# Mean squares and inverse roots of blocks 2 to 7: from TensorE to GpSimd and VectorE

## The chip, the cores and the metric

One core of a Trainium2 chip runs the whole program as one launch. The metric is the device time of that launch in microseconds; the median of three runs is compared. The engines have a queue each and run side by side: TensorE (PE in the profile; its weight loads are PEld), VectorE (DVE), ScalarE (ACT), GpSimd (POOL). SyncE (SP) issues nearly all the transfers. They meet at semaphores only.

## The reference, cut to what matters

`x` has 2 batches of 2048 tokens and 512 features. Two layers follow each other:

```python
# layer 0
scale = cond @ norm_w.T + 1.0
ms = jnp.mean(x * x, axis=-1, keepdims=True)
h = x * (scale[:, None, :] * jax.lax.rsqrt(ms + EPS))
u = h @ up_w.T                      # 512 -> 4096
val, gate = jnp.split(u, 2, axis=-1)
h = val * jax.nn.gelu(gate, approximate=False)
y = act_quant(h) @ weight_quant(down_w).T + x
# layer 1: down = relu(y @ Wd_b.T + bd); out = y + down @ Wu_b.T + bu
```

`Wd_b` and `Wu_b` are weights that are made from the condition by two large products with `cond`. The change concerns the second and third line of layer 0 alone: the mean square of each token, and the inverse root that all 512 features of the token are multiplied by.

## The kernel before, in words

Features lie on the 128 partitions and tokens along the free dimension. The 4096 tokens are 8 blocks of 512 (`TB`); two blocks make a stage `s` (0 to 3). The up projection of a stage is done in 16 steps `j`, 64 in all (`n = 16 s + j`, called quads in the code). A quad is seven products of block matrices (a Winograd-like scheme, `product(n, p)` in the order 1, 5, 3 of the quad before, 6, 4 of the quad before, 2, 7); a product is six 128x128 by 128x512 matmuls in f16, since each operand is split in a high and a low half. Between the quads stand the groups for the layer-1 weights (`adapter_group`, 16 matmuls), the down projection of the stage before (`down`), and small products.

The order of the work on each engine is written out by hand, in one loop over the quads for each engine. What a quad needs from the others:

- `product(n, 5)` waits in stage 0 for `u_low(n, 1)` on VectorE (the low half of part 1 of the weights), and behind every second quad for `exponents` (the scales of the next two quads' weights).
- `product(n, 7)` waits for `seed_c(n)` on VectorE.
- In stage 0 the split weights of quad `j` are made while quad `j - 1` runs: GpSimd makes four sums of weight blocks (`weight_sums(j)`, four additions of 128x256), ScalarE rounds them (`u_high(j, 1)` from the first two sums, `u_high(j, 3)` from the last two), VectorE makes the low halves (`u_low`). From stage 1 on they are loaded from DRAM.
- ScalarE's order in quad `n` of stage 0 is `seed_b(n)`, `keep_p5(n)`, `u_high(n+1, 0)`, `gate2(n-1)`, `u_high(n+1, 1)`, `absolute2(n-1)`, `row_sums(n+3)`, `absolute1(n-1)`, `u_high(n+1, 2)`, `u_high(n+1, 3)`, `gate1(n)`.
- VectorE's order in it ends with `u_low(n+1, 0)`, `multiply2(n-1)`, `seed_c(n)`, `multiply1(n-1)`, `running_max2(n-1)` (which waits for `absolute2`), `running_max1(n-1)` (which waits for `absolute1`), `u_low(n+1, 1)`, `val2(n)`.

The rows of the next stage are prepared in quads 2 to 15 of the stage that runs. For each of its two blocks: ScalarE squares the four groups of features and VectorE adds them up in `res[:, 2, :]` (`add_squares`). Behind quad 6 (first block) and quad 9 (second), `stat` on TensorE sums over the partitions, by four f32 matmuls of the squares with a column of ones, into four columns of `e_ps`, with the tokens now on the partitions; `mean_square` on VectorE reads them at the start of the next quad, and product 5 waits for that. At the end of quad 10, `rsqrt` makes the roots of both blocks, 128 x 4 each. Behind quads 11 and 12, `spread_rs` on TensorE turns them back by four transposes into one 128x512 PSUM bank, in which every partition has the root of every token, and `x_scaled` on VectorE multiplies the block by it at the start of quads 12 and 13.

GpSimd has one queue: `weight_sums` of all 16 steps in `SUM_ORDER`, and then `all_h(s)`, two `partition_all_reduce` over the running maxima, once a stage. Blocks 0 and 1 have a path of their own, which the change leaves alone.

Of the kernel before, what the change touches and what calls it, by code (L numbers as in the profile page):

```python
# [165 lines left out]
STAT = {6: 0, 9: 1}  # L166
ROOTS = 10
SPREAD = {11: 0, 12: 1}
NEXT_X = {2: 0, 5: 1}
MID_AT = {49: 0, 52: 1, 55: 2}  # L170
UP_AT = {n + 1 + k // 2: (i, (k, k + 1)) for n, i in MID_AT.items() for k in (0, 2)}
# [6 lines left out]
def side_work(n):  # L178

    s, j = divmod(n, NP)  # L180
    work = [("dw", g) for g in groups_of_quad(n)]
    if n == 0:
        work.append(("bounds", 0))
    if s + 1 < NSB:
        if j in SPREAD:
            work.append(("rs", 2 * s + 2 + SPREAD[j]))
    if s > 0 and Y_FIRST <= j < Y_FIRST + 4:
        for m in (2 * (j - Y_FIRST), 2 * (j - Y_FIRST) + 1):
            work.append(("y", 2 * (s - 1) + m // KD, m % KD))
    if n in MID_AT:  # L190
        work.append(("mid", MID_AT[n]))
    if n in UP_AT:
        i, ks = UP_AT[n]
        work += [("up", i, k) for k in ks]
    return work
# [20 lines left out]
def build(nc, x, cond, norm_w, up_w, down_w, Wd, bd, Wu, bu, Wdd, bdd, Wdu, bdu, out):  # L216
    aux = aux_plan()
    aux_keys = list(aux)
    with ExitStack() as ctx:
# [46 lines left out]

        d_raw = res[:, 0:2, :].rearrange("p a t -> p (a t)")
        norm_raw = stage[:, 0, :]
        cs_pow = exps[:, 0:B]
        h_half = h_ring[:, :, :].rearrange("p s t -> p (s t)").bitcast(F16).rearrange(  # L270
            "p (s t) -> p s t", s=SLOTS)
# [143 lines left out]
        s_sqp = sem("s_sqp")  # L415
        s_rs = sem("s_rs")
        s_spread = sem("s_spread")
        s_xs = sem("s_xs")
        s_t = [sem(f"s_t_sum{m}") for m in range(7)]
        s_thi = sem("s_thi")  # L420
# [12 lines left out]
        s_wq = sem("s_wq")  # L433
        s_mean = sem("s_mean")
        s_down_total = sem("s_down_total")
        s_stat = sem("s_stat")
        s_stage = sem("s_stage")
        s_l1w = sem("s_l1w")
        s_chain = sem("s_chain")
# [7 lines left out]
        def bank_free(key):  # L447
            kind, i = key[:2]
            at = ADAPTERS.index(i) if kind in ("mid", "up") else 0
            return {  # L450
                "scale": (s_cs, 1),
                "stat": (s_ms, 1),
                "rs": (s_xs, KD * (i + 1)),
                "total": (s_top, 1),
                "bounds": (s_top, bound_count(3)),
                "dw": (s_stage, i + 1),
                "y": (s_x1, KD * i + key[-1] + 1),
                "mid": (s_relu, at + 1),
                "up": (s_out, KD * at + key[-1] + 1),
            }[kind]  # L460
# [246 lines left out]
        @block.gpsimd  # L707
        def _(pool):
            pool.memset(ones[:, :], 1.0).then_inc(s_const, 1)
            pool.memset(ident[:, :], 1.0).then_inc(s_const, 1)  # L710
            pool.wait_ge(s_const, 2)
            pool.affine_select(out=ident[:, :], in_=ident[:, :], compare_op=ALU.is_equal, fill=0.0,
                               base=0, pattern=[[-1, P]], channel_multiplier=1).then_inc(s_const, 1)

            def a_block(j, half, which):
                return u_raw(j)[:, 2 * half:2 * half + 2, P * which:P * which + P]

            def weight_sums(j):

                pool.wait_ge(s_u[j % 4], 16 * (j // 4 + 1))  # L720
                if j == 2:

                    aux_ready(pool, "dw", 2)
                elif j == 4:
                    aux_ready(pool, "dw", 3)
                elif j == 0:

                    pool.wait_ge(s_seed_c, 1)
                elif j >= 3:
                    if j == 6:  # L730
                        pool.wait_ge(s_sums_lo, 2)
                    pool.wait_ge(s_ulo, part_count(j - 2, 3))
                s1, s2, s3, s4 = (s_sum(j, n, n + 1).rearrange("p (k m) -> p k m", k=2)
                                  for n in range(4))
                pool.tensor_tensor(s1, a_block(j, 0, 0), a_block(j, 1, 0), ALU.add)\
                    .then_inc(s_us, 1)
                pool.wait_ge(s_us, sum_count(j, 1))
                pool.tensor_tensor(s2, s1, a_block(j, 0, 1), ALU.subtract).then_inc(s_us, 1)
                pool.tensor_tensor(s3, a_block(j, 0, 1), a_block(j, 0, 0), ALU.subtract)\
                    .then_inc(s_us, 1)  # L740
                pool.wait_ge(s_us, sum_count(j, 2))
                pool.tensor_tensor(s4, a_block(j, 1, 1), s2, ALU.subtract).then_inc(s_us, 1)

            def all_h(s):

                if s:
                    pool.wait_ge(s_x1, 2 * KD * s)
                for t, s_max in ((1, s_max2), (0, s_max1)):
                    pool.wait_ge(s_max, NP * (s + 1))
                    if s == NSB - 1 and t == 0:  # L750

                        pool.wait_ge(s_step, 1)
                    pool.partition_all_reduce(yscale[:, TB * t:TB * t + TB],  # L753
                                              hmax[:, TB * t:TB * t + TB], P, AR.absmax)\
                        .then_inc(s_ma[t], 1)


            pool.wait_ge(s_rs, 2)
            for j in SUM_ORDER:
                weight_sums(j)  # L760
            for n in range(NP, NQ, NP):
                all_h(n // NP - 1)
            all_h(NSB - 1)

        @block.scalar
        def _(act):
# [6 lines left out]
            def square(i, k):  # L773
                act.wait_ge(s_x[i % 2], 16 * (i // 2))
                if k == 0 and i % 2:
                    act.wait_ge(s_stat, i - 2)
                if k > 1:
                    act.wait_ge(s_sqp, (KD - 1) * (i - 2) + k - 1)
                act.activation(res[:, 2 + (k > 0), :], x_sb[:, i % 2, k, :], ACT.Square)\
# [239 lines left out]
        def _(pe):  # L1019
# [16 lines left out]
            def product(n, p):  # L1036
# [14 lines left out]
                elif p == 5:  # L1051
# [3 lines left out]
                        pe.wait_ge(s_top, bound_count(2))  # L1055
                    if n - 1 in BOUND_QUADS:
                        pe.wait_ge(s_top, bound_count(n + 1))
                    if stat_of_quad(n - 1) is not None:
                        pe.wait_ge(s_ms, stat_of_quad(n - 1) + 1)
                    if n - 1 == MEAN_QUAD:  # L1060
                        pe.wait_ge(s_mean, 1)
                    ps = e_ps
# [76 lines left out]
                                   start=True, stop=True)  # L1139
                mm.then_inc(s_aux, 1)  # L1140

            def stat(i):
                ps = e_ps[:, 2:2 + NT] if i else take("stat", 0)
                if i == 0:
                    pe.wait_ge(s_sqr, KD - 1)
                    sq = h_ring[:, 0, 0:TB]
                else:
                    pe.wait_ge(s_sqp, (KD - 1) * (i - 1))
                    sq = res[:, 2, :]
                for t in range(NT):  # L1150
                    mm = pe.matmul(ps[:, t:t + 1], sq[:, P * t:P * t + P], ones[:, 0:1],
                                   start=True, stop=True)
                mm.then_inc(s_stat if i else s_aux, 1)

            def stat1(part):

# [6 lines left out]
                mm.then_inc(s_stat1, 1)  # L1163

            def spread_rs(i):
                ps = spread_first[i] if i < 2 else take("rs", i)
                pe.wait_ge(s_rs, i + 1)
                for t in range(NT):
                    col = NT * (i % 2) + t
                    mm = pe.transpose(ps[:, P * t:P * t + P],  # L1170
                                      rs[:, (i // 2) % 2, col:col + 1].to_broadcast([P, P]),
                                      ident[:, :])
                mm.then_inc(s_spread if i < 2 else s_aux, 1)

            def down(i, k):
                ps = take("y", i, k)
# [68 lines left out]
                               cond_sb[:, 0:B], start=True, stop=True)  # L1245
            mm.then_inc(s_aux, 1)
            pe.wait_ge(s_const, 1)
            stat(0)
            stat1(0)
            first_bounds()  # L1250
            pe.wait_ge(s_const, 3)
# [21 lines left out]
            for n in range(NQ):  # L1273
# [9 lines left out]
                    product(n, 7)  # L1283
                for g in groups_of_quad(n):
                    adapter_group(g)
                if stat_of_quad(n) is not None:
                    pe.wait_ge(s_p5sb, n)
                    stat(stat_of_quad(n))
                if n in BOUND_QUADS:
                    pe.wait_ge(s_p5sb, n)  # L1290
                    bounds(n + 2, n + 3, e_ps).then_inc(s_total, 1)
# [1 line left out]
                    pe.wait_ge(s_p5sb, n)  # L1293
                    down_total()
                for key in side_work(n)[len(groups_of_quad(n)):]:
                    if key[0] == "rs":
                        spread_rs(key[1])
                    elif key[0] == "bounds":
                        bounds(3, 3, take(*key)).then_inc(s_aux, 1)
                    elif key[0] == "y":  # L1300
                        down(key[1], key[2])
# [46 lines left out]
        def _(dve):  # L1348
# [108 lines left out]
            def mean_square(i):  # L1457
# [6 lines left out]
                        total, e_ps[:, 0:2 * NT].rearrange("p (k t) -> p t k", k=2),  # L1464
                        AX_X, ALU.add))
                elif i:
                    dve.wait_ge(s_stat, i - 1)
                    total = e_ps[:, 2:2 + NT]
                else:
                    aux_ready(dve, "stat", 0)  # L1470
                    total = bank("stat", 0)[:, 0:NT]
# [3 lines left out]
            def rsqrt(i, count=1):  # L1475
# [4 lines left out]
                if i == 0:  # L1480
# [19 lines left out]
                dve.scalar_tensor_tensor(out=y, in0=t, scalar=1.5 * 1.5, in1=y,  # L1500
                                         op0=ALU.add, op1=ALU.mult).then_inc(s_rs, count)

            def x_scaled(i, ks=range(KD)):
                if i < 2:
                    dve.wait_ge(s_spread, i + 1)
                    roots = spread_first[i]
                else:
                    aux_ready(dve, "rs", i)
                    roots = bank("rs", i)
                b = i // 4  # L1510
                for k in ks:
                    xk = x_sb[:, i % 2, k, :]
# [251 lines left out]
            for n in range(1, NQ):  # L1764
# [15 lines left out]
                for key in side_work(n - 1):  # L1780
                    if key[0] == "y":
                        residual(key[1], (key[2],))
                    elif key[0] == "rs":
                        x_scaled(key[1])
                    elif key[0] == "up":
                        finish(key[1], key[2])
                if j == 0:
                    t_low(s, T3)
                if s + 1 < NSB:
# [56 lines left out]
                    t_low(s + 1, B21)  # L1846
                if j == ROOTS and s + 1 < NSB:
                    rsqrt(2 * s + 2, 2)
                if n == 12:
                    down_mean()  # L1850
            n = NQ - 1
# [92 lines left out]
```

## Time and profile before

| | us |
|---|---|
| median of three runs | 850.98 (849.87, 850.98, 851.22) |
| span of the profiled execution, first to last instruction | 847.8 |
| TensorE busy | 834.7 |
| VectorE busy | 605.6 |
| ScalarE busy | 388.4 |
| GpSimd busy | 74.3 |

The times of whole runs hold some microseconds more than the span, before the first and after the last instruction; the profile tells nothing of those. Busy times add up each engine's instructions; a busy TensorE is not yet a TensorE at its peak, since matmuls overlap and their ends are modelled. What a matmul costs in the flow is read from the distance of two starts.

### The profile page before, as it was taken

Reading aid. Unit: us, or ns where it says so; the run is one execution under the profiler, and the core shown is the slowest. Engines: PE = TensorE matmul, PEld = TensorE weight load, DVE = VectorE, ACT = ScalarE, POOL = GpSimd, SP = SyncE. Lnnn points to the kernel's source line nnn. Section 1 sums busy time; section 2 is a strip of 40 time slices with the busy share of each in tenths; the row PEclk is TensorE's granted clock in tenths of the full one; section 3 lists DMA queues with packets and bytes.
Section 4 is the critical chain, followed back from the end, with each engine's and each line's share of the span. In section 5 each row is a group of like instructions: output and inputs, shape, how many; then the busy total and the mean of one; then the engine's idle time right before and its main releaser. Section 6 shows DMA issues by size and latency. Waiting matters only on the chain.

```text
span 847.8 us, 11801 instructions
## 1 busy us (share of the span) xinstructions
PE 834.7 (98%) x3982; PEld 366.9 (43%) x3982; DVE 605.6 (71%) x904; ACT 388.4 (46%) x633; POOL 74.3 (9%) x79
## 2 busy tenths in 40 slices
PE   6999999999999999999999999999999999999998
PEld 4334444444444444444444444444444444444443
DVE  5998787989877765658776656668975664445986
ACT  5778887775454532237454542126333332224000
POOL 0363332202000000002000000000200000000100
PEclk9999999999999999999999999999999999999999
DMA  9879988665999843377889754436246444432232
GB/s 342 333 269 339 348 285 300 235 224 209 323 350 373 305 149 117 116 255 274 294 308 335 270 200 134 151 106 211 84 133 217 137 162 141 140 117 77 99 123 76
DMA packets 64426, 183.49 MB, mean 216 GB/s; under 512 B 7024, under 2 KB 8304, under 8 KB 64368
## 3 DMA queue, kind: packets, MB, share of 16 engines
q1 hardware_dynamic: 64080, 182.48, 61.7%
q8 instruction: 33, 0.54, 0.2%
q10 hardware_dynamic: 288, 0.26, 0.1%
q14 instruction: 25, 0.20, 0.1%
HBM read 152.31 MB, written 29.36 MB: 214 GB/s over the span
## 4 chain that ended last, share of the span: by engine, by line
PE 93%; DVE 1%; issue 0%; DVEq 0%
PE aux_ps L1182 10%; PE b_ps L1082 9%; PE b_ps L1086 9%; PE b_ps L1084 9%; PE a_ps L1082 6%; PE a_ps L1086 6%; PE a_ps L1084 6%; PE aux_ps L1137 6%; PE aux_ps L1233 3%; PE aux_ps L1224 3%; PE c_ps L1086 3%; PE c_ps L1082 3%; PE c_ps L1084 3%; PE e_ps L1082 3%; PE e_ps L1086 3%; PE e_ps L1084 3%
## 5 line engine op out<-in xcount | busy, mean ns | idle before, releaser
L1590 DVE SCALAR_TENSOR_TENSOR h_ring<-v_sb,unscale,gelu 128x512 f32<-128x512 f32 x63 | 50.9, 808 | 101.2 <-ACT gelu L885 53.4
L861 ACT ACTIVATE b_ps<-a_ps 128x512 f32<-128x512 f32 x63 | 36.7, 583 | 140.4 <-PE a_ps L1086 140.3
L1082 PE MATMUL b_ps<-t_mov,u_l 128*128 128x512 f16 x252 | 95.5, 379 | 0.6 <-DVE c_ps L1551 0.6
L1086 PE MATMUL b_ps<-t_mov,u_l 128*128 128x512 f16 x252 | 95.5, 379 | 0.0
L1084 PE MATMUL b_ps<-t_mov,u_l 128*128 128x512 f16 x252 | 95.5, 379 | 0.0
L1614 DVE TENSOR_TENSOR hmax<-gelu,hmax 128x512 f32<-128x512 f32 x120 | 82.8, 691 | 7.6 <-ACT gelu L891 2.5
L1182 PE MATMUL aux_ps<-h_ring,wq 128*128 128x512 f16 x384 | 84.8, 379 | 0.0
L753 POOL PARTITION_ALL_REDUCE yscale<-hmax x8 | 17.9, 2266 | 601.3 <-DVE hmax L1614 600.7
L895 ACT ACTIVATE gelu<-h_ring 128x512 f32<-128x512 f32 x64 | 40.3, 630 | 56.5 <-DVE h_ring L1590 56.5
L891 ACT ACTIVATE gelu<-h_ring 128x512 f32<-128x512 f32 x64 | 40.2, 629 | 52.5 <-DVE h_ring L1600 52.4
L1600 DVE SCALAR_TENSOR_TENSOR h_ring<-b_ps,unscale,gelu 128x512 f32<-128x512 f32 x64 | 47.9, 749 | 18.9 <-PE b_ps L1086 18.7
L877 ACT ACTIVATE gelu<-a_ps,unscale 128x512 f32<-128x512 f32 x64 | 43.6, 682 | 37.5 <-DVE hmax L1614 35.2
L885 ACT ACTIVATE gelu<-c_ps,unscale 128x512 f32<-128x512 f32 x64 | 43.9, 686 | 32.9 <-PE c_ps L1086 32.9
L1137 PE MATMUL aux_ps<-w_ring,cond_sb 128*32 128x512 f32 x480 | 58.1, 599 | 0.0
L1182 PEld LDWEIGHTS aux_ps<-h_ring,wq 128*128 128x128 fp8e4 x384 | 37.6, 98 | 44.4
L1647 DVE TENSOR_TENSOR h_ring<-h_ring,qscale 128x1024 f16<-128x1024 f32 x48 | 56.5, 1217 | 0.0
L868 ACT ACTIVATE p_sb<-e_ps 128x512 f32<-128x512 f32 x63 | 37.5, 595 | 37.2 <-PE e_ps L1086 27.4
L1559 DVE TENSOR_TENSOR v_sb<-b_ps,p_sb 128x512 f32<-128x512 f32 x63 | 43.3, 688 | 14.1 <-PE b_ps L1086 13.9
L1673 DVE TENSOR_TENSOR aux_ps<-aux_ps,yscale 128x512 f32<-128x512 f32 x24 | 16.8, 700 | 44.8 <-PE aux_ps L1182 41.5
L1082 PE MATMUL b_ps<-t_mov,u_e 128*128 128x512 f16 x126 | 47.8, 379 | 1.0 <-DVE t_mov L1543 1.0
L1082 PE MATMUL e_ps<-t_mov,u_e 128*128 128x512 f16 x126 | 47.8, 379 | 0.2 <-DVE u_e L1399 0.2
L1082 PE MATMUL a_ps<-t_mov,u_e 128*128 128x512 f16 x126 | 47.9, 380 | 0.0
(225 smaller groups left out, 1620.0 us busy)
## 6 DMA issues: line engine op xcount, KB each, us to landing
w_ring<-in_Wdu SPq DMA_DIRECT2D x64, 512.0 KB, 6.1
w_ring<-in_Wdd SPq DMA_DIRECT2D x56, 512.0 KB, 6.9
u_l<-ul_dram SPq DMA_DIRECT2D x48, 512.0 KB, 4.5
u_e<-ue_dram SPq DMA_DIRECT2D x48, 384.0 KB, 3.1
h_ring<-in_up_w SPq DMA_DIRECT2D x16, 512.0 KB, 6.7
x_sb<-in_x SPq DMA_DIRECT2D x8, 1024.0 KB, 8.0
res<-in_down_w SPq DMA_DIRECT2D x16, 512.0 KB, 7.1
ul_dram<-u_l SPq DMA_DIRECT2D x15, 512.0 KB, 5.6
```

The lines of the kernel that those rows point to most:

```text
L877: act.activation(gelu1[:, :], a_ps[n % 2][:, :], ACT.Gelu, scale=unscale[:, s // 2, j:j + 1]).then_inc(s_g1, 1)
L885: act.activation(gelu2[:, :], c_ps[:, :], ACT.Gelu, scale=unscale[:, s // 2, j:j + 1]).then_inc(s_g2, 1)
L1082: pe.matmul(ps[:, :], weight(n, p, 0, k), hi, start=fresh and k == 0, stop=False, skip_group_check=True)
L1084: pe.matmul(ps[:, :], weight(n, p, 0, k), lo, start=False, stop=False, skip_group_check=True)
L1086: mm = pe.matmul(ps[:, :], weight(n, p, 1, k), hi, start=False, stop=k == 1, skip_group_check=True)
L1137: mm = pe.matmul(ps[32 * q:32 * q + 32, :], cond_sb[:, :], w_tile(n)[:, 512 * (q % 2):512 * (q % 2) + 512], start=True, stop=True)
L1182: mm = pe.matmul(ps[:, :], wq[:, c, P * k:P * k + P], q_slot(s, c)[:, TB * t:TB * t + TB], start=(c == 0), stop=(c == NP - 1))
L1559: dve.tensor_tensor(v_sb[:, :], b_ps[n % 2][:, :], p5_sb[:, :], ALU.add)\
L1590: dve.scalar_tensor_tensor(out=h_slot(n)[:, TB:TS], in0=val[:, :], scalar=unscale[:, s // 2, j:j + 1], in1=gelu2[:, :], op0=ALU.mult, op1= ...
L1600: dve.scalar_tensor_tensor(out=h_slot(n)[:, 0:TB], in0=b_ps[n % 2][:, :], scalar=unscale[:, s // 2, j:j + 1], in1=gelu1[:, :], op0=ALU.mul ...
L1614: dve.tensor_tensor(total, absolute, total, ALU.max).then_inc(done, 1)
L1647: dve.tensor_tensor(q_slot(s, c), h_slot(NP * s + c), qscale[:, :], ALU.mult)\
```

## The change

For blocks 2 to 7, TensorE's `stat` and `spread_rs` go. In their place:

- `square_total(i)` on GpSimd: a `partition_all_reduce` (add) of `res[:, 2, :]` into `res[:, 3, :]`, which leaves every token's sum on every partition. In stage 0 it stands behind `weight_sums(7)` (block 2) and `weight_sums(10)` (block 3), in stages 1 and 2 behind `all_h`.
- `mean_square(i)` on VectorE multiplies this 128x512 grid by the unit matrix, repeated four times, and sums each group of 128: the sums come to lie on the partitions of the tokens.
- `spread_roots(i)` on VectorE multiplies the unit matrix by the roots into `res[:, 3, :]`: for block 2s+2 behind `rsqrt` at the end of quad 10, for block 2s+3 behind `x_scaled(2s+2)`.
- `root_rows(i)` on GpSimd: a second `partition_all_reduce` (add) of this into `res[:, 2, :]`. In stage 0 it stands behind `weight_sums(12)` (block 2) and `weight_sums(13)` (block 3). `x_scaled` reads this instead of the PSUM bank.
- Product 5 no longer waits for `s_ms`; ScalarE's second square of an odd block waits for it, since it writes `res[:, 3, :]`.

```diff
+TOTAL_BEHIND = {7: 2, 10: 3}
+ROWS_BEHIND = {12: 2, 13: 3}
...
-    if s + 1 < NSB:
-        if j in SPREAD:
-            work.append(("rs", 2 * s + 2 + SPREAD[j]))
...
+        root_grid = res[:, 3, :].rearrange("p (t q) -> p t q", t=NT)
+        diagonal = ident[:, :].unsqueeze(1).to_broadcast([P, NT, P])
...
+            def square_total(i):
+
+                pool.wait_ge(s_sqp, (KD - 1) * (i - 1))
+                pool.partition_all_reduce(res[:, 3, :], res[:, 2, :], P, AR.add)\
+                    .then_inc(s_square_total, 1)
+
+            def root_rows(i):
+
+                pool.wait_ge(s_root_grid, i - 1)
+                pool.wait_ge(s_xs, KD * i)
+                pool.partition_all_reduce(res[:, 2, :], res[:, 3, :], P, AR.add)\
+                    .then_inc(s_root_rows, 1)
+
             pool.wait_ge(s_rs, 2)
             for j in SUM_ORDER:
                 weight_sums(j)
-            for n in range(NP, NQ, NP):
-                all_h(n // NP - 1)
+                if j in TOTAL_BEHIND:
+                    square_total(TOTAL_BEHIND[j])
+                if j in ROWS_BEHIND:
+                    root_rows(ROWS_BEHIND[j])
+            for s in range(1, NSB):
+                all_h(s - 1)
+                if s + 1 < NSB:
+                    for t in range(2):
+                        square_total(2 * s + 2 + t)
+                    for t in range(2):
+                        root_rows(2 * s + 2 + t)
             all_h(NSB - 1)
...
                 if k == 0 and i % 2:
-                    act.wait_ge(s_stat, i - 2)
+                    act.wait_ge(s_square_total, i - 2)
+                if k == 1 and i % 2:
+                    act.wait_ge(s_ms, i)
...
-                    if stat_of_quad(n - 1) is not None:
-                        pe.wait_ge(s_ms, stat_of_quad(n - 1) + 1)
...
-                if stat_of_quad(n) is not None:
-                    pe.wait_ge(s_p5sb, n)
-                    stat(stat_of_quad(n))
...
-                    if key[0] == "rs":
-                        spread_rs(key[1])
-                    elif key[0] == "bounds":
+                    if key[0] == "bounds":
...
-                    dve.wait_ge(s_stat, i - 1)
-                    total = e_ps[:, 2:2 + NT]
+
+                    dve.wait_ge(s_square_total, i - 1)
+                    total = ms_half[:, col:col + NT]
+                    link(dve.tensor_tensor(root_grid, root_grid, diagonal, ALU.mult))
+                    link(dve.tensor_reduce(total, root_grid, AX_X, ALU.add))
...
+            def spread_roots(i):
+
+                col = NT * (i % 2)
+                dve.wait_ge(s_rs, 2 * (i // 2) + 2)
+                if i % 2:
+                    dve.wait_ge(s_root_rows, i - 2)
+                dve.tensor_tensor(root_grid, diagonal,
+                                  rs[:, (i // 2) % 2, col:col + NT].unsqueeze(2)
+                                  .to_broadcast([P, NT, P]), ALU.mult).then_inc(s_root_grid, 1)
...
-                    aux_ready(dve, "rs", i)
-                    roots = bank("rs", i)
+                    dve.wait_ge(s_root_rows, i - 1)
+                    roots = res[:, 2, :]
...
+                if s + 1 < NSB and j - 1 in SPREAD:
+                    x_scaled(2 * s + 2 + SPREAD[j - 1])
+                    if SPREAD[j - 1] == 0:
+                        spread_roots(2 * s + 3)
...
                 if j == ROOTS and s + 1 < NSB:
                     rsqrt(2 * s + 2, 2)
+                    spread_roots(2 * s + 2)
```

## Rows read from the trace of the kernel before

**Rows 1.** The page: busy time by engine; the chain that ended last, by engine.
```profile
PE 834.7 (98%) x3982; PEld 366.9 (43%) x3982; DVE 605.6 (71%) x904; ACT 388.4 (46%) x633; POOL 74.3 (9%) x79
...
PE 93%; DVE 1%; issue 0%; DVEq 0%
```

**Rows 2.** Waits of TensorE: total us, times, longest.
```profile
PE b_ps L1082 <- DVE c_ps L1551: 0.6, 1, 0.6
```

**Rows 3.** Timeline of TensorE: start us, duration us, line, operation.
```profile
17.28 0.63 PE L1120 MATMUL a_ps<-t_mov,u_e 128*128 128x512 f16 x1
...
109.55 0.38 PE L1082 MATMUL a_ps<-t_mov,u_e 128*128 128x512 f16 x1
...
129.86 0.95 PE L1151 MATMUL e_ps<-ones,res 128*128 128x1 f32 x8
130.67 0.38 PE L1082 MATMUL a_ps<-t_mov,u_e 128*128 128x512 f16 x1
...
143.22 0.38 PE L1082 MATMUL e_ps<-t_mov,u_e 128*128 128x512 f16 x1
...
150.99 0.60 PE L1170 MATMUL aux_ps<-ident,rs 128*128 128x128 f32 x4
151.43 0.38 PE L1082 MATMUL a_ps<-t_mov,u_e 128*128 128x512 f16 x1
...
163.15 0.38 PE L1082 MATMUL a_ps<-t_mov,u_e 128*128 128x512 f16 x1
...
172.21 0.38 PE L1082 MATMUL a_ps<-t_mov,u_e 128*128 128x512 f16 x1
```

**Rows 4.** Timeline of GpSimd; idle time before, and its releaser, in brackets.
```profile
0.93 0.20 POOL L710 MEMSET ident<- 128x128 f32 x1
10.99 0.28 POOL L712 TENSOR_SCALAR_AFFINE_SELECT ident<-ident 128x128 f32<-128x128 f32 x1 [9.86 <-issue]
21.62 0.73 POOL L735 TENSOR_TENSOR yscale<-h_ring 128x256 f32<-128x256 f32 x1 [10.35 <-DVE rs L1500]
...
84.49 0.91 POOL L742 TENSOR_TENSOR yscale<-h_ring,yscale 128x256 f32<-128x256 f32 x1
92.23 1.04 POOL L735 TENSOR_TENSOR h_ring<-h_ring 128x256 f32<-128x256 f32 x1 [6.82 <-DVE u_l L1399]
...
112.03 1.21 POOL L735 TENSOR_TENSOR h_ring<-h_ring 128x256 f32<-128x256 f32 x1 [5.20 <-DVE u_l L1399]
...
201.22 4.56 POOL L753 PARTITION_ALL_REDUCE yscale<-hmax  x2 [32.88 <-DVE hmax L1614]
```

**Rows 5.** Timeline of ScalarE in quad 7: rounding of part 1 for quad 8.
```profile
105.15 0.71 ACT L815 ACTIVATE u_e<-h_ring,um_mul 128x512 f16<-128x512 f32 x1
```

**Rows 6.** Timeline of VectorE in quads 6 to 14.
```profile
92.00 0.68 DVE L1535 TENSOR_TENSOR res<-res 128x512 f32<-128x512 f32 x1
...
109.21 0.74 DVE L1399 SCALAR_TENSOR_TENSOR u_e<-h_ring,um_mul,u_e 128x512 f16<-128x512 f32 x1
...
140.07 0.68 DVE L1559 TENSOR_TENSOR v_sb<-b_ps,p_sb 128x512 f32<-128x512 f32 x1
...
142.83 0.17 DVE L1361 TENSOR_SCALAR exps<-exps 128x2 int32<-128x2 int32 x1
...
165.20 2.72 DVE L1513 SCALAR_TENSOR_TENSOR x_sb<-aux_ps,cs_x,x_sb 128x512 f32<-128x512 f32 x4
169.20 0.68 DVE L1551 TENSOR_TENSOR c_ps<-b_ps,p_sb 128x512 f32<-128x512 f32 x1
```

**Rows 7.** VectorE beside an idle and beside a reducing GpSimd; groups by line.
```profile
197.34 1.22 DVE L1543 TENSOR_TENSOR t_mov<-h_ring,t_mov 128x1024 f16<-128x1024 f32 x1
...
201.79 2.19 DVE L1543 TENSOR_TENSOR t_mov<-x_sb,t_mov 128x1024 f16<-128x1024 f32 x1
...
L753 POOL PARTITION_ALL_REDUCE yscale<-hmax x8 | 17.9, 2266 | 601.3 <-DVE hmax L1614 600.7 <-DVE yscale L1867 0.6
L1614 DVE TENSOR_TENSOR hmax<-gelu,hmax 128x512 f32<-128x512 f32 x120 | 82.8, 691 | 7.6 <-ACT gelu L891 2.5
```

More of the change, by code:

```diff
@@ L417, in build @@
         s_spread = sem("s_spread")
+        s_square_total = sem("s_square_total")
+        s_root_grid = sem("s_root_grid")
+        s_root_rows = sem("s_root_rows")
         s_xs = sem("s_xs")
@@ L435, in build @@
         s_down_total = sem("s_down_total")
-        s_stat = sem("s_stat")
         s_stage = sem("s_stage")
@@ L452, in bank_free @@
                 "stat": (s_ms, 1),
-                "rs": (s_xs, KD * (i + 1)),
-                "total": (s_top, 1),
+                    "total": (s_top, 1),
                 "bounds": (s_top, bound_count(3)),
@@ L1140, in adapter_group, with stat0 @@
                 mm.then_inc(s_aux, 1)
[L1142 to L1149, printed above, removed]
+            def stat0():
+                ps = take("stat", 0)
+                pe.wait_ge(s_sqr, KD - 1)
+                sq = h_ring[:, 0, 0:TB]
                 for t in range(NT):
@@ L1152, in stat @@
                                    start=True, stop=True)
-                mm.then_inc(s_stat if i else s_aux, 1)
+                mm.then_inc(s_aux, 1)
             def stat1(part):
@@ L1165, in spread_rs @@
             def spread_rs(i):
-                ps = spread_first[i] if i < 2 else take("rs", i)
+                ps = spread_first[i]
                 pe.wait_ge(s_rs, i + 1)
                 for t in range(NT):
-                    col = NT * (i % 2) + t
+                    col = NT * i + t
                     mm = pe.transpose(ps[:, P * t:P * t + P],
-                                      rs[:, (i // 2) % 2, col:col + 1].to_broadcast([P, P]),
-                                      ident[:, :])
-                mm.then_inc(s_spread if i < 2 else s_aux, 1)
+                                      rs[:, 0, col:col + 1].to_broadcast([P, P]), ident[:, :])
+                mm.then_inc(s_spread, 1)
             def down(i, k):
@@ L1247, in _ @@
             pe.wait_ge(s_const, 1)
-            stat(0)
+            stat0()
             stat1(0)
@@ L1782, in _ @@
                         residual(key[1], (key[2],))
-                    elif key[0] == "rs":
-                        x_scaled(key[1])
                     elif key[0] == "up":
                         finish(key[1], key[2])
+                if s + 1 < NSB and j - 1 in SPREAD:
+                    x_scaled(2 * s + 2 + SPREAD[j - 1])
+                    if SPREAD[j - 1] == 0:
+                        spread_roots(2 * s + 3)
                 if j == 0:
```

## The prediction, made before the changed kernel was run

> **What bounds the kernel now.** I read the page first: TensorE is busy 98% of the span and holds 93% of the chain that ended last [rows 1]. The list of its waits agrees: behind the opening it waits for VectorE for fractions of a microsecond, the longest 0.6 us [rows 2]. So TensorE sets the time, and what is taken from it comes back in full, unless something new makes it wait. The rest is a reading of timelines, first TensorE's for the price of the small products, then GpSimd's, ScalarE's and VectorE's in stage 0, because there VectorE and GpSimd work to a deadline in every quad.
>
> **What is removed.** `stat` of block 3 starts at 129.86 and the next quad at 130.67: 0.81 us [rows 3]. The five others stand behind an adapter group or before a `bounds` and take 0.92 each in the same timeline: 5.4 us. `spread_rs` of block 2 takes from 150.99 to 151.43: 0.44 us [rows 3]; six are 2.6 us. Sum removed from TensorE: **8.0 us**. The three stages' shares: 1.7 + 0.9 in stage 0, and 5.4 us in stages 1 and 2, where a quad leaves VectorE idle for 2 to 3 us and GpSimd stands idle (it waits 601 us in all for VectorE [rows 7]), so that nothing there takes the gain back.
>
> **What VectorE gets.** A multiply of 128x512 costs 0.69 us [rows 7]. `mean_square` gets one, and a reduce of 128x512 that no row shows: between 0.15 (a tiny instruction, like the 0.17 in rows 6) and 1.4 (twice the multiply); I take 0.7, since it reads the same elements. `spread_roots` is one multiply. Together 2.1 us for a block, 12.5 us in all. In stages 1 and 2 idle time covers it. In stage 0 two places have no cover. `exponents` behind quad 10 end at 142.83 + 0.17 = 143.00, and product 5 of quad 11 starts at 143.22 [rows 3, 6]: 0.2 us of room, and `spread_roots` puts 0.7 ahead: a wait of 0.5. `seed_c(13)` ends at 169.88, and product 7 of quad 13 starts 36 matmuls of 0.216 behind 163.15, at 170.9: 1.0 us of room, of which the earlier TensorE and a contended `x_scaled(3)` (below) take 0.5 to 3. Quad 12 lies between. Alone, these waits make 1 to 4 us of the 8.0.
>
> **Contention.** A VectorE instruction with two inputs in SBUF takes 1.22 us alone and 2.19 beside a `partition_all_reduce` [rows 7]: up to 1.0 lost for each of the 12 new reductions, of which four lie in stage 0. `x_scaled` now reads both inputs from SBUF and meets the additions of `weight_sums(15)`. This is in the 1 to 4 us above.
>
> **What GpSimd gets, and in which order.** A reduction takes 2.27 us [rows 7]; for ADD no row stands, the nearest is this absolute maximum, and even 4.5 would fit. The four in stage 0 would delay `weight_sums(8)` and the following by about 3 us, and they have that. What decides is something else: in the kernel before, GpSimd changes its kind of work only three times. From MEMSET to AFFINE_SELECT the profile shows 9.86 us in which it waits for nothing (`issue`), though its only input was ready at 1.13. To the first addition it waits 10.35 us and to the first reduction 32.88 us for VectorE [rows 4], so that a cost of changing the code there would be hidden. The change alternates additions and reductions: total 2 behind sums 7, total 3 behind 10, rows 2 behind 12, rows 3 behind 13, each with additions behind it: eight changes of kind, in a queue that feeds every quad. I price one at L = 9.86, the only such gap in the trace; bounds: 0 and, since transfers load the start as much as stage 0, 11.
>
> The Trainium skill speaks against the change in the same way ("GPSIMD Engine Reference", section "Instruction dispatch"): GpSimd's routines are loadable, and the first call of a freshly loaded one pays about 6 us in which the profile shows no instruction. The trace's gap is 9.86 us, longer; by the page's 6 us the sum below would come out near 848 us, and by the row near 873.
>
> **The sum at L = 9.86.** Times are those of the timeline before. A `weight_sums` takes 3.6 us (additions of 0.73 to 1.21 [rows 4]), its first half 1.8. When its first half is late at U, ScalarE's `u_high(j, 1)`, `absolute2`, `row_sums`, `absolute1` and VectorE's `running_max1`, `u_low(j, 1)` follow before product 5: before, 109.21 - 105.15 + 0.74 = 4.8 [rows 5, 6], of which 0.5 was waiting for other things, so 4.3.
> - Sums 7 end at 85.4 [rows 4]; change 95.3 (the squares are ready at 92.7 [rows 6]); reduction 97.6; change 107.5; sums 8 have U = 109.3 where ScalarE wanted it at 105.15 [rows 5]. Product 5 of quad 8 starts at 113.6, not 109.55 + 1.30 = 110.85: now 2.75 late.
> - Sums 9 end at 114.7, sums 10 (ready 112.03 + 2.75) at 118.4; change 128.3; reduction 130.6; change 140.5; U(11) = 142.3, `val2(10)` at 146.6; from it to the end of `exponents` were 2.93 us (140.07 to 143.00 [rows 6]), now 3.6. Product 5 of quad 11 at 150.2, not 143.22: 7.0 late.
> - Sums 12 end at 147.7; change 157.6; reduction 159.9; change 169.8; U(13) = 171.6, + 4.3 + 1.2 (`val2`, `exponents`): product 5 of quad 13 at 177.1, not 163.15 + 1.30: 12.7 late.
> - Sums 13 end at 173.4; change 183.3; reduction 185.6. Here `x_scaled(3)` waits for it at the head of VectorE's queue, with `multiply2` and `seed_c(13)` behind it: 4.7 us from its start to the end of `seed_c` (165.20 to 169.88 [rows 6]): product 7 at 190.3, not 170.9: 19.4 late.
> - Change 195.5; U(14) = 197.3, + 3.2 (no `row_sums` in quad 13): product 5 of quad 14 at 200.5, not 172.21 + 1.30: **27.0 late**. Sums 15 are in time, and the last reduction code is loaded before stage 0 ends.
>
> Against this stand the 5.4 us of stages 1 and 2; stage 0's 2.6 are in the chain. 27.0 - 5.4 = +21.6: the span 847.8 becomes 869.4. The median of the runs is 3.2 above the span of the profile, which I carry over: **872 us**.
>
> The chain is steep in L, since six or seven changes stand on it: the same steps give 853 at L = 7, 858 at 8, 882 at 11. From 6.6 downwards the slack takes nearly all, and the change is faster.
>
> **The rivals.**
> - *The changes of kind are free (or up to 6 us).* For: the 9.86 us gap stands at the start of the program and could be a matter of the start; nothing else in the trace shows a load. Against: the queue's MEMSETs ran at 0.3 to 1.1 us and the gap came behind them. Then the waits of VectorE's additions remain: 851 - 8.0 + 1 to 4 = 844 to 847, **846 us**, faster. It decides from L = 6.6 down. Chance 0.13.
> - *Changes of 6.4 to 6.8 us:* gain and loss cancel, **851 us**. Chance 0.03.
> - *The clock falls in the new gaps.* TensorE stands for some 5 to 9 us in quads 11, 13 and 14. The granted clock is full in every stretch of the profile, so no row shows a fall; in the opening, where TensorE has gaps, an f16 matmul took 0.63 us, not 0.38 [rows 3]. At half speed for 3 us behind each of three gaps the cost is up to 5 us, part of it hidden behind VectorE: **875 to 877 us**, on top of the forecast. Chance 0.2, inside the forecast's range.
>
> **How the numbers follow.** Changes of kind on the path: 0.84, forecast 872, its own range 855 to 885 (L from 7.5 to 11, or the clock). Free or cheap: 0.13, 846. Cancelled: 0.03. The range of 8 in 10 takes the first case and its lower edge down to L = 7: 853 to 885. What a measurement can tell from no change is about 0.2% (1.7 us). Faster 0.13, same 0.03, slower 0.84.
>
> **What would show it.** In GpSimd's timeline of stage 0, gaps of about 10 us with no releaser before each of the four reductions and before sums 8, 11, 13 and 14; ScalarE waiting for GpSimd before `u_high` of parts 1; VectorE waiting for GpSimd before `x_scaled(3)`; TensorE idle in quads 8, 11, 13 and 14 and nowhere else; stages 1 and 2 shorter by 5.4 us with TensorE without waits; no `stat` and `spread_rs` rows beyond those of blocks 0 and 1; the new multiplies at 0.7 us. It is wrong if GpSimd passes from additions to reductions without a gap (then 846), if such a change costs less towards reductions than the first one did, or if the reduction with ADD is much dearer than 2.27 us.

## The result, and the profile after

| | us |
|---|---|
| before, median | 850.42 (849.67 to 851.22) |
| after, median | 869.12 (867.8 to 869.65) |
| ratio | 1.0222, 95% interval 1.0208 to 1.0237: slower |
| forecast | 872, range 853 to 885 |

The profiled execution of the changed kernel took 867.8 us, of which the span is 866.0, 18.2 more than the 847.8 of before. The page of the changed kernel, busy times and the chain that ended last (to hold against [rows 1]):

```profile
PE 833.9 (96%) x3910; PEld 359.1 (41%) x3910; DVE 631.9 (73%) x922; ACT 387.9 (45%) x633; POOL 118.3 (14%) x91
...
PE 78%; issue 8%; DVE 4%; POOL 3%; ACT 1%; DVEq 0%; POOLq 0%; ACTq 0%
```

TensorE has 72 instructions fewer and still ends later. Its share of the chain fell from 93% to 78%, and "issue", time in which an engine waits for nothing that the profile shows, holds 8%. GpSimd's timeline shows where that is (start, duration, and in brackets the idle time before; the additions between are left out, except the last before and the first behind each reduction):

```profile
84.83 0.91 POOL L744 TENSOR_TENSOR yscale<-h_ring,yscale 128x256 f32<-128x256 f32 x1
94.66 3.25 POOL L763 PARTITION_ALL_REDUCE res<-res  x1 [8.93 <-DVE u_e L1413]
105.45 0.72 POOL L737 TENSOR_TENSOR h_ring<-h_ring 128x256 f32<-128x256 f32 x1 [7.54 <-issue]
...
116.40 0.91 POOL L744 TENSOR_TENSOR h_ring<-h_ring 128x256 f32<-128x256 f32 x1
125.73 3.25 POOL L763 PARTITION_ALL_REDUCE res<-res  x1 [8.42 <-DVE res L1562]
138.65 0.71 POOL L737 TENSOR_TENSOR yscale<-h_ring 128x256 f32<-128x256 f32 x1 [9.66 <-issue]
...
153.25 3.25 POOL L770 PARTITION_ALL_REDUCE res<-res  x1 [7.62 <-DVE u_e L1413]
164.44 0.96 POOL L737 TENSOR_TENSOR yscale<-h_ring 128x256 f32<-128x256 f32 x1 [7.94 <-issue]
...
174.09 3.25 POOL L770 PARTITION_ALL_REDUCE res<-res  x1 [6.00 <-issue]
186.32 0.71 POOL L737 TENSOR_TENSOR h_ring<-h_ring 128x256 f32<-128x256 f32 x1 [8.98 <-issue]
```

Before each of the eight changes of kind GpSimd stands for 6.0 to 9.7 us. One of the gaps is a wait for data: the squares of block 3 are ready at 125.6, and the reduction begins at 125.73. The other seven end later than their data came (block 2's squares are ready at 93.0, 1.7 us before the reduction), and their mean is 8.1. In [rows 4] there is one such gap, 9.86 us, at the start. A reduction with ADD takes 3.25 us, not the 2.27 of the absolute maximum [rows 7].

What hangs on the late additions is in TensorE's waits (total us, times, longest), to hold against [rows 2]:

```profile
PE e_ps L1106 <- DVE u_e L1413: 8.0, 2, 6.5
PE b_ps L1106 <- DVE c_ps L1578: 6.7, 5, 2.9
...
PE e_ps L1106 <- DVE exps L1375: 4.4, 1, 4.4
```

The large ones have the place that the forecast named: `u_low` in front of product 5 of quads 8 and 14, `exponents` in front of product 5 of quad 11, `seed_c` in front of product 7 of quad 13 (2.9 us). The other four waits for `seed_c` stand in quad 2 (0.5; 0.6 in the kernel before), in quad 12 (1.2), and in quads 44 and 45 (1.6 and 0.4), where the forecast had none. In front of product 5 of quad 13, where it had one, TensorE does not wait. TensorE's timeline against the forecast's chain:

| TensorE instruction | before | forecast | after |
|---|---|---|---|
| quad 8, product 5 | 110.85 | 113.6 | 111.90 |
| quad 11, product 5 | 143.22 | 150.2 | 148.75 |
| quad 13, product 5 | 164.44 | 177.1 | 172.35 |
| quad 13, product 7 | 170.9 | 190.3 | 181.93 |
| quad 14, product 5 | 173.5 | 200.5 | 192.75 |
| quad 15, product 1 | 183.47 | | 204.61 |

```profile
111.90 0.39 PE L1106 MATMUL e_ps<-t_mov,u_e 128*128 128x512 f16 x1 [1.46 <-DVE u_e L1413]
...
148.75 0.55 PE L1106 MATMUL e_ps<-t_mov,u_e 128*128 128x512 f16 x1 [4.40 <-DVE exps L1375]
...
181.93 0.38 PE L1106 MATMUL b_ps<-t_mov,u_l 128*128 128x512 f16 x1 [2.94 <-DVE c_ps L1578]
...
192.75 0.61 PE L1106 MATMUL e_ps<-t_mov,u_e 128*128 128x512 f16 x1 [6.52 <-DVE u_e L1413]
```

Two of these matmuls take 0.55 and 0.61 us, not 0.38. The busy times by stretch (TensorE, its weight loads, VectorE, ScalarE, GpSimd; then the granted clock and the transfers) show why:

```profile
143.00:148.70 5.70, 1.35 (x7) 0.39 (x4) 5.13 (x17) 4.34 (x9) 2.63 (x3) 1.00 0.33 70
148.70:152.70 4.00, 3.95 (x11) 1.50 (x12) 2.16 (x9) 0.99 (x2) 0.00 (x0) 0.57 0.78 226
...
183.00:192.70 9.70, 3.23 (x8) 0.88 (x6) 3.50 (x4) 4.01 (x7) 6.23 (x8) 0.68 0.00 0
192.70:197.00 4.30, 4.25 (x11) 1.56 (x12) 4.20 (x6) 1.14 (x3) 0.57 (x1) 0.54 0.56 217
```

Behind the two longest waits the granted clock is 0.57 and 0.54, which is most of the stretch at the lower of the two levels (1.2 and 2.4 GHz). At (1 - clock) times the stretch that is an estimated 1.7 and 2.0 us of TensorE's time in addition to the waits. The starts agree: from product 5 of quad 11 to the start of quad 12 TensorE's delay grows from 5.5 to 6.8 us, where `spread_rs` should have taken 0.4 off it, and from product 5 of quad 14 to the start of quad 15 it grows from 19.2 to 21.1. Only the second counts in the end. Product 5 of quad 14 waits for sums 14, and between the slow stretch of quad 11 and sums 14 GpSimd's queue waits for no data: what TensorE loses in quad 11 only makes its later waits shorter.

Quad by quad, TensorE is 21.1 us late at the start of quad 15. In stages 1 and 2 it wins back 0.76 to 0.92 at each `stat` and 0.44 at each `spread_rs` up to quad 44. At quads 45 and 46 stand steps of +1.33 and +0.58 where -0.44 and 0 were due: 2.4 us lost. At quad 46 it is 18.3 late, and it ends there.

### The profile page after: what moved, and what is told of

It reads as the page before. It is cut to its first block, busy times and chain, and to the rows that moved or that the text cites. A ratio compares the mean times of both kernels' runs of the same rounds, so it can differ in the third digit from the quotient of the medians.

```text
span 866.0 us, 11702 instructions
## 1 busy us (share of the span) xinstructions
PE 833.9 (96%) x3910; PEld 359.1 (41%) x3910; DVE 631.9 (73%) x922; ACT 387.9 (45%) x633; POOL 118.3 (14%) x91
## 4 chain that ended last, share of the span: by engine, by line
PE 78%; issue 8%; DVE 4%; POOL 3%; ACT 1%; DVEq 0%; POOLq 0%; ACTq 0%
PE aux_ps L1201 10%; PE b_ps L1106 8%; PE b_ps L1108 8%; PE b_ps L1110 8%; PE a_ps L1106 5%; PE aux_ps L1161 5%; PE a_ps L1110 5%; PE a_ps L1108 5%; PE aux_ps L1252 3%; PE aux_ps L1243 3%; PE e_ps L1106 3%; PE e_ps L1110 3%; PE e_ps L1108 3%; PE c_ps L1108 3%; PE c_ps L1110 3%
## 5 line engine op out<-in xcount | busy, mean ns | idle before, releaser
L1641 DVE TENSOR_TENSOR hmax<-gelu,hmax 128x512 f32<-128x512 f32 x120 | 85.9, 719 | 18.3 <-ACT gelu L921 10.6
L1674 DVE TENSOR_TENSOR h_ring<-h_ring,qscale 128x1024 f16<-128x1024 f32 x48 | 64.7, 1388 | 0.0
L1106 PE MATMUL e_ps<-t_mov,u_e 128*128 128x512 f16 x126 | 48.8, 387 | 12.4 <-DVE u_e L1413 8.0
L1110 PE MATMUL e_ps<-t_mov,u_e 128*128 128x512 f16 x126 | 48.8, 388 | 0.0
```

The lines of the kernel that those rows point to most:

```text
L1106: pe.matmul(ps[:, :], weight(n, p, 0, k), hi, start=fresh and k == 0, stop=False, skip_group_check=True)
L1110: mm = pe.matmul(ps[:, :], weight(n, p, 1, k), hi, start=False, stop=k == 1, skip_group_check=True)
L1641: dve.tensor_tensor(total, absolute, total, ALU.max).then_inc(done, 1)
L1674: dve.tensor_tensor(q_slot(s, c), h_slot(NP * s + c), qscale[:, :], ALU.mult)\
```

## The experiments

Theory K: GpSimd's changes of kind (from additions to a reduction or back) in stage 0 cost the time. Rival V: VectorE's added work, and its contention with the reductions, cost it in every stage. Rival R: the reductions themselves, 3.25 us each, cost it. The kernel before ran beside each group on the same chip: 850.12 in the first, 850.04 in the second, 849.80 in the third.

**Stages 1 and 2 alone, and stage 0 alone.** A constant chooses the stages whose rows take the new path (2 and 3 in the first run, 1 in the second); the others keep `stat` and `spread_rs`.

```diff
+NEW = (2, 3)
...
+def old_stat(n):
+
+    i = stat_of_quad(n)
+    return i is not None and i // 2 not in NEW
...
-                if s + 1 < NSB and j - 1 in SPREAD:
+                if s + 1 < NSB and s + 1 in NEW and j - 1 in SPREAD:
```

> Blocks 2 and 3 (prepared in stage 0) take the old path through TensorE, blocks 4 to 7 the new one, so GpSimd passes from additions to reductions once, as before. Theory K (the changes of kind on GpSimd in stage 0 cost the time): what is left is the gain of stages 1 and 2, 5.4 us, less the 1.9 us that the changed kernel's quads 44 and 45 lost: 850.4 - 5.4 + 1.9 = 847. Rival V (VectorE's added work and its contention with reductions cost it, in every stage alike): 18.7 us of loss over three stages, so two of them leave 850.4 + 12 = 862. Quad by quad, K expects 0 at quad 15, V a third of the loss.

Measured: 846.53 us (846.24 to 847.6), ratio 0.996 (0.9947 to 0.9972). K said 847, V 862.

> The reverse: only blocks 2 and 3 take the new path. Theory K: the whole loss without the later gain, 869.1 + 5.4 - 1.9 = 872.6 us, quad 15 at +21 us. Rival V: a third of the loss, 850.4 + 6 = 857.

Measured: 872.84 us (872.02 to 875.06), ratio 1.0271 (1.0255 to 1.0287). K said 872.6, V 857. The two parts add up: -3.6 and +22.7 make +19.1, the whole change made +18.7. All of the loss is stage 0's, and V falls as the main cause.

**Tiny reductions and tiny additions in the kernel before.** They change nothing but GpSimd's queue; the second has the same places and the same semaphores as the first.

```diff
             for j in SUM_ORDER:
                 weight_sums(j)
+                if j in (7, 10, 12, 13):
...
+                    pool.partition_all_reduce(probe[:, 0:2], ones[:, 0:2], P, AR.add)
```

> The kernel before, with a partition_all_reduce of 128x2 into a tile that nobody reads behind sums 7, 10, 12 and 13: the computation is unchanged, VectorE gets nothing to do and nothing waits for these reductions. Theory K: eight changes of kind; with 8 us towards a reduction and 8.5 back, sums 8, 11 and 13 just make it (first half at 104, 135, 159) and sums 14 do not: first half at 179.4, product 5 of quad 14 at 182.6 instead of 173.5, about +9 us: 859. Rival V: an unread reduction of 128x2 costs nothing: 850.4. Rival R (the reductions themselves are the load, 3.25 us each): 850.4 as well, since these are tiny.

Measured: 856.38 us (852.86 to 862.19 in 10 runs), ratio 1.0074 (1.0052 to 1.0095). The profiled execution was one of the quickest, and its GpSimd timeline reads:

```profile
84.47 0.91 POOL L744 TENSOR_TENSOR yscale<-h_ring,yscale 128x256 f32<-128x256 f32 x1
94.85 0.41 POOL L767 PARTITION_ALL_REDUCE probe<-ones  x1 [9.48 <-issue]
104.85 0.72 POOL L737 TENSOR_TENSOR h_ring<-h_ring 128x256 f32<-128x256 f32 x1 [9.59 <-issue]
...
161.91 0.51 POOL L767 PARTITION_ALL_REDUCE probe<-ones  x1 [5.79 <-issue]
169.43 1.17 POOL L737 TENSOR_TENSOR h_ring<-h_ring 128x256 f32<-128x256 f32 x1 [7.02 <-issue]
```

A reduction of 0.41 us, on inputs that lay ready from the start, has 9.48 us of nothing ahead and 9.59 behind. K said 859. The gaps are there without long reductions and without a wait for data, and they alone cost 6.3 us: R falls as the cause by itself. The gaps vary from 5.8 to 9.6 us within this one execution. The time of a run varies by 9 us, that of the kernel before by 2; that the gaps' size makes this difference is likely but not shown, since one execution was profiled.

R does not fall as a part of the loss. Sums 14 start at 169.43 in this run and at 186.32 in the changed kernel. Counted from the end of sums 7 (85.38 and 85.74), 16.5 us lie between the two: the four reductions are 11.3 us longer (13.0 in all, not 1.7), the eight gaps are 5.8 longer (65.1, not 59.3), and the additions are a little shorter. Product 5 of quad 14 starts 16.4 us later (192.75, not 176.34). So the gaps use up the slack of the queue, and behind them the reductions' length counts in full. No run has long reductions without gaps; that they would be harmless then is the forecast's argument from the slack, and not shown.

> The same with a tensor_tensor addition of 128x2 in place of each reduction; the computation is unchanged. Theory K: no change of kind, 850.4 us. A rival by which any instruction inserted in GpSimd's queue delays the sums would show the same time as with the tiny reductions.

Measured: 849.68 us (849.26 to 851.1 in 10 runs), ratio 0.9998 (0.9989 to 1.0008). The inserted addition follows the last of the sums without a gap:

```profile
85.00 0.92 POOL L744 TENSOR_TENSOR yscale<-h_ring,yscale 128x256 f32<-128x256 f32 x1
85.88 0.64 POOL L767 TENSOR_TENSOR probe<-ones 128x2 f32<-128x2 f32 x1
92.74 1.04 POOL L737 TENSOR_TENSOR h_ring<-h_ring 128x256 f32<-128x256 f32 x1 [6.23 <-DVE u_l L1406]
```

It is the kind, not an instruction more in the queue. What GpSimd does in such a gap no row shows.

**The removal alone.** `stat` and `spread_rs` are gone and nothing stands in their place.

```diff
             def square_total(i):
+                return
...
-                    link(dve.tensor_tensor(root_grid, root_grid, diagonal, ALU.mult))
-                    link(dve.tensor_reduce(total, root_grid, AX_X, ALU.add))
+                    total = res[:, 2, 0:NT]
```

> What TensorE's share is worth by itself: stat and spread_rs of blocks 2 to 7 are gone and nothing replaces them. It leaves out the sums over partitions and the spreading: mean_square takes four columns of the added squares, x_scaled multiplies by whatever lies in the squares' tile. Both theories: the removed 8.0 us come back in full, 850.1 - 8.0 = 842.1, with at most 0.5 lost in quad 13, where x_scaled now has two inputs in SBUF beside GpSimd's additions. If TensorE were held by something else already, it would stay above 845.

Measured: 843.97 us (843.45 to 845.41), ratio 0.9928 (0.9916 to 0.9940): 6.1 us, not 8.0, and 1.9 above what was expected. TensorE's steps of 0.80 to 0.92 and 0.44 are there; 1.2 are lost in quad 12, 0.2 in quad 14, and 0.6 in quad 45. VectorE's timeline in quad 12:

```profile
151.57 4.15 DVE L1537 SCALAR_TENSOR_TENSOR x_sb<-res,cs_x,x_sb 128x512 f32<-128x512 f32 x4
155.64 0.94 DVE L1413 SCALAR_TENSOR_TENSOR u_e<-h_ring,um_mul,u_e 128x256 f16<-128x256 f32 x1
```

Four instructions of `x_scaled(2)`, now with both inputs in SBUF, take 4.15 us beside the additions of `weight_sums(14)`; in [rows 6] four with one input in PSUM take 2.72.

**The removal with VectorE's work.**

```diff
             def square_total(i):
+                return
...
             def root_rows(i):
+                return
```

> The same with VectorE's new work back (two multiplies of 128x512 and one reduce a block, at their places), but without GpSimd's reductions: VectorE works on unsummed squares and x_scaled on an unsummed tile. The forecast's step for VectorE without cover: a wait of 0.5 us in front of product 5 of quad 11 and up to 1 us in quads 12 and 13, so 842.1 + 0.5 to 1.5 = 842.6 to 843.6. Rival V (VectorE's extra work alone costs a large part) expects over 846.

Measured: 844.99 us (844.86 to 846.58), ratio 0.9944 (0.9931 to 0.9957): 1.0 more than the removal alone, which is the 0.5 to 1.5 that was expected on top of it. The sum 842.6 to 843.6 was missed, since the removal alone had not come to 842.1, and V's 846 is only 1.0 away from the median. The ranges of the two runs overlap; the traces decide. They show a wait of 0.5 us for `exponents` in quad 11 that was not there, and one of 1.7 instead of 1.1 for `seed_c` in quad 12. Without GpSimd's reductions the change would be faster by 5 us, so VectorE's own work is not what made it slower.

**The totals alone in stage 0.**

```diff
 TOTAL_BEHIND = {7: 2, 10: 3}
-ROWS_BEHIND = {12: 2, 13: 3}
+ROWS_BEHIND = {}
```

> Of the new path only the totals of blocks 2 and 3 (square_total behind sums 7 and 10, mean_square by the unit matrix); their roots go through TensorE's transposes, and stages 1 and 2 are the kernel before. Four changes of kind instead of eight. By the forecast's chain the places behind sums 7 and 10 cost what quad 12 shows in the changed kernel, 6.8 us, less 0.7 for the missing spread_roots: 850.1 + 6.1 = 856. So the two places of root_rows, behind sums 12 and 13, carry the larger part, some 15 us. If every excursion cost the same, this would be half of the loss, about 861.

Measured: 858.63 us (858.47 to 860.03), ratio 1.0106 (1.0092 to 1.0119): +8.8, where the chain with the changed kernel's gaps gave +6. In this run the three gaps that are no wait for data were 10.4, 6.9 and 10.8 us, a mean of 9.4 against 8.7 at the same places there. That the places differ in price is in keeping with the trace, but the time alone does not settle it: half of the loss would have been 861, and 858.6 lies between. Held against the run with stage 0 alone (+22.7), the two places of `root_rows` add 13.9 us, more than the 8.8 of the first two; but they act on a queue that the first two have already made late.

**Where spread_roots and x_scaled stand.** In the run with stages 1 and 2 alone, the steps of +1.33 and +0.58 at quads 45 and 46 are still there. VectorE's timeline of the changed kernel there, with GpSimd's reduction:

```profile
551.99 0.74 DVE L1540 SCALAR_TENSOR_TENSOR x_sb<-res,cs_x,x_sb 128x512 f32<-128x512 f32 x1
554.63 0.69 DVE L1526 TENSOR_TENSOR res<-ident,rs 128x512 f32<-128x512 f32 x1
...
555.95 2.61 DVE L1740 SCALAR_TENSOR_TENSOR l_wd<-l_wd,w_ring 128x512 f32<-128x512 f32 x1
...
555.41 3.60 POOL L770 PARTITION_ALL_REDUCE res<-res  x1 [20.95 <-DVE res L1526]
```

The second instruction of `assemble`, with two inputs in SBUF, takes 2.61 us beside the reduction; the same instruction of the kernel before takes 0.69, at 536.30. The first of two runs moves `spread_roots` of the second block behind `val2`:

```diff
-                    if SPREAD[j - 1] == 0:
-                        spread_roots(2 * s + 3)
...
                 val2(n)
+                if s + 1 < NSB and s + 1 in NEW and SPREAD.get(j - 1) == 0:
+                    spread_roots(2 * s + 3)
```

> Blocks 4 to 7 on the new path as in the run with stages 1 and 2 alone, and spread_roots of the second block of a stage moved from behind x_scaled to behind val2 of the same quad, so that its reduction no longer runs beside assemble, whose second instruction took 2.6 instead of 0.7 us. If the 1.9 us lost in quads 44 and 45 come from that contention, 846.5 - 1.9 = 844.6; if from the added VectorE time itself, it stays at 846.5.

Measured: 845.40 us (844.92 to 847.75), ratio 0.9948 (0.9936 to 0.9959): 1.1 less than 846.53, between the two expected times, and the intervals of the two ratios overlap. What shows is in the trace: the step of 1.33 at quad 45 became -0.44, the one of 0.57 at quad 46 stayed. The latter has another cause, and the order of VectorE's work suggests it: in the kernel before, `x_scaled` stood ahead of the two residuals of its quad and filled the wait for the down projection; the change moved it behind them, where it delays `assemble` and `seed_c`. The next run puts it back:

```diff
+                if s + 1 < NSB and s + 1 in NEW and j - 1 in SPREAD:
+                    x_scaled(2 * s + 2 + SPREAD[j - 1])
+                    if SPREAD[j - 1] == 0:
+                        spread_roots(2 * s + 3)
                 for key in side_work(n - 1):
                     if key[0] == "y":
```

> As the run with stages 1 and 2 alone, but x_scaled and spread_roots stand ahead of the residuals in VectorE's quads 12 and 13, where x_scaled stood in the kernel before (the change had put it behind them). Theory: in quads 44 and 45 the waits for the down projection's banks cover x_scaled again, and the reduction runs beside the residuals, which have one input in SBUF each, and not beside assemble; then all of the 5.4 us comes back: 850.1 - 5.4 = 844.7, with no step in quads 45 and 46. If the loss there has another cause, it stays between 845.4 and 846.5, and the step of 0.57 at quad 46 stays.

Measured: 844.95 us (843.69 to 845.65), ratio 0.9938 (0.9925 to 0.9952). The steps at quads 45 and 46 are gone, which bears out both causes. VectorE's timeline in quad 45: no wait ahead of the first residual, and `assemble` at 0.69 again.

```profile
540.12 2.73 DVE L1587 SCALAR_TENSOR_TENSOR x_sb<-res,cs_x,x_sb 128x512 f32<-128x512 f32 x4
542.96 0.70 DVE L1747 TENSOR_TENSOR aux_ps<-aux_ps,yscale 128x512 f32<-128x512 f32 x1
...
548.47 0.69 DVE L1787 SCALAR_TENSOR_TENSOR l_wd<-l_wd,w_ring 128x512 f32<-128x512 f32 x1
```

This version, which takes the new path for blocks 4 to 7 only, is faster than both kernels: 4.9 us (0.6%) under its own 849.80 of before. Its time and that of the run before it overlap, so the second repair is shown by the steps in the traces and not by the medians.

## Why the prediction was right, step by step

- **What bounds the kernel.** Right. TensorE without waits gave back what was taken from it at each place: 0.76 to 0.92 for `stat`, 0.44 for `spread_rs`.
- **The gain.** 8.0 us forecast; the removal alone brought 6.1. The rest went to two things that come with it: `x_scaled` with two inputs in SBUF, and its new place behind the residuals.
- **VectorE's extras.** The reduce that no row showed takes 0.686 us (0.7 taken), the multiplies 0.684 and 0.688. They cost 1.0 us by the medians. With the slower `x_scaled` of quad 12, the profiled execution without reductions loses 2.7 us in stage 0, inside the 1 to 4 forecast, and the part that should leave 844 to 847 without GpSimd left 845.0.
- **The changes of kind.** The mechanism was right and the price too high: L = 9.86 was the only gap in the trace, the seven measured ones have a mean of 8.1. By the forecast's chain that alone would have given 859. The Trainium skill's figure of about 6 us for the first call of a freshly loaded routine ("GPSIMD Engine Reference", section "Instruction dispatch") is the lower end of what the runs show between additions and reductions, 5.8 to 10.8; the traces agree that no instruction shows in such a gap. That it is a loading of code, no run shows.
- **The sum.** At product 5 of quad 14 the forecast had TensorE 27.0 us late, and it was 19.2: 7.8 less. The eight gaps came to 65.1 us and not to 78.9, which is 13.8 less. Against this, the four reductions of 3.25 and not 2.27 put 3.9 on, and the way from the first half of sums 14 (done at 187.83) to product 5 took 4.9 us and not 3.2, for the most part because VectorE's work there ran beside the additions of sums 15:

```profile
189.20 2.36 DVE L1641 TENSOR_TENSOR hmax<-gelu,hmax 128x512 f32<-128x512 f32 x2 [6.77 <-ACT gelu L921]
191.48 1.21 DVE L1413 SCALAR_TENSOR_TENSOR u_e<-h_ring,um_mul,u_e 128x512 f16<-128x512 f32 x1
```

  The same instructions take 1.47 and 0.74 us in quad 13 of the kernel before. Small differences of other terms make the last 0.4.
- **What came on top.** Behind quad 14's wait the half clock cost 1.9 us, and quads 44 and 45 lost 2.4. The forecast's own terms, 869.4 + 3.2, make 872.6, written as 872; 872.6 - 7.8 + 1.9 + 2.4 = 869.1, the measured time. So the mechanism was right, and the closeness of the number in part luck: one price was too high by 13.8 us in all, and four were too low or missing by 9.9.
- **A step that failed:** "In stages 1 and 2 idle time covers it", "so that nothing there takes the gain back". At quad 44, `assemble` fills that idle time, and `x_scaled` had left the wait that covered it. In stages 1 and 2 this took 2.4 us of the 5.4.
- **The offset.** 3.2 us between the span of the profile and the median; measured 869.12 - 866.0 = 3.1. Right, though only 1.8 of it lie outside the span: the profiled execution was also the quickest of the four, 1.3 under the median.
- **The rivals.** Free changes of kind (846): refuted by the tiny reductions. Changes of 6.4 to 6.8 us (851): single gaps are that short, their mean is not. The falling clock: it came, behind two of the three waits with a cost that can be told. The 3 us at half speed behind each gap stand in no row of before; measured are stretches of 4.0 and 4.3 us at 0.57 and 0.54, an estimated 3.7 us, of which one wait hid 1.7.

## What to carry to other kernels

Before work is given to an idle GpSimd, list its queue by kind of operation: here each change between additions and reductions cost more (5.8 to 10.8 us) than the reduction itself (3.25), and is hidden only where the queue had to wait that long anyway, so a kind belongs at one end of the queue or in stages that use no other. An idle gap marked "issue" before the first instruction of a kind is a price to be used, with a range: the next one may differ by some us. A long operation that fits into the slack can still count in full once a gap has used the slack up. Where an instruction is moved in an in-order queue, ask what wait it used to fill.

## What the runs showed of the hardware that was not expected

- A `partition_all_reduce` of 128x512 f32 takes 3.25 us with ADD and 2.27 with the absolute maximum; at 279.21, beside two VectorE instructions of 128x1024 with two inputs in SBUF, 4.14. One of 128x2 takes 0.41 to 0.51.
- The gap at a change of kind varies from 5.8 to 10.8 us between places and executions. It begins when the queue reaches it, not when the inputs are ready, so part of it overlaps a wait for data: at 117.3 the queue was free, the squares came at 125.6, and the reduction began 0.1 us later, so that hardly anything of the change was left to pay.
- A VectorE instruction with two inputs in SBUF beside a reduction: 2.61 us instead of 0.69. The Trainium skill ("SBUF — State Buffer", section "Who interferes with whom") says that a VectorE instruction with two inputs in SBUF contends with a GpSimd instruction that reads SBUF, and calls the ports they share an exclusive lock. The trace agrees on the contention. A lock held for the whole reduction is not what it shows: VectorE's instruction ended at 558.56, 1.9 us later than alone, and the reduction ran from 555.41 to 559.01.
- The additions of `weight_sums` slow VectorE as well: four instructions with two inputs in SBUF take 4.15 us beside them in quad 12 and 2.73 in quad 13 of the same run.
